# Three first additions of the closing stage move from VectorE to TensorE, and the last group's two loads signal apart

## What is computed

```python
x = x + xattn(ctx_1024, ctx_1024, layernorm(x), ...)      # softmax attention over 64 keys
def ffn(x, ...):                                          # E = 8 experts, K = 2, F = 512
    probs, idx = top_k(softmax(xt @ Wr + br), K)          # divided by their sum
    h = layernorm(relu(xt @ W1[e] + b1[e])) * g1 + be1
    y = layernorm(relu(h @ W2[e] + b2[e])) * g2 + be2
    out[t] = sum over k of gate[t, k] * y[idx[t, k], t]
x = x + ffn(layernorm(x), ...)
```

## Time and profile before

| what | us |
|---|---|
| median of 3 runs | 329.74 |
| lowest, highest run | 328.38, 334.85 |
| span of the profiled execution | 284.0 |
| TensorE, VectorE busy in the span | 240.0, 237.6 |
| ScalarE, POOL busy in the span | 215.7, 189.0 |

### The profile page before, as it was taken

How to read it: one execution, slowest core, us unless ns; L and a number is a source line. 1 busy time by engine, 2 the same in 40 slices (tenths; PEclk the granted TensorE clock), 3 DMA queues, 4 the chain that set the end, 5 groups by cost and what they waited for, 6 DMA issues and landing times.

```text
span 284.0 us, 10362 instructions
## 1 busy us (share of the span) xinstructions
PE 240.0 (84%) x2955; PEld 196.8 (69%) x2958; DVE 237.6 (84%) x1101; ACT 215.7 (76%) x799; POOL 189.0 (67%) x301
## 2 busy tenths in 40 slices
PE   1899779699798398769879999999999699889970
PEld 1474568567676244669768989999999599879520
DVE  0765986965997987778989899999999879889896
ACT  2544666779859867757799999999999789889820
POOL 8601277777667757827768777878887758677650
PEclk9977986999779759988999999999999999999997
DMA  6997398123424154351223333333235746452338
GB/s 162 336 265 256 77 270 261 48 86 102 124 77 158 49 85 104 80 133 48 60 51 67 78 69 69 58 80 77 61 78 152 142 132 141 125 141 58 106 117 289
DMA packets 48803, 34.59 MB, mean 122 GB/s; under 512 B 26934, under 2 KB 42870, under 8 KB 48747
## 3 DMA queue, kind: packets, MB, share of 16 engines
q1 hardware_dynamic: 39100, 22.83, 30.1%
q0 software_dynamic: 6592, 9.00, 11.9%
q10 hardware_dynamic: 3056, 2.11, 2.5%
HBM read 15.14 MB, written 12.02 MB: 96 GB/s over the span
## 4 chain that ended last, share of the span: by engine, by line
PE 22%; DVE 18%; issue 16%; POOL 14%; DMA 12%; ACT 8%; SPq 6%; POOLq 1%; DVEq 1%; ACTq 0%
PE bank L724 14%; POOL answers L682 9%; PE bank L728 7%; POOL words_of L708 5%; DMA w2f<-in_L_ffn_W 3%; DMA answers<-vo,words_of 3%; SPq L522 3%; DMA x_tok<-in_x 2%; DVE w2f L1668 2%; SPq L554 2%; DMA w_mean<-w_sums 1%; DMA kb_room<-slot_rows 1%; ACT ex L1175 1%; ACT xt L1198 1%; ACT rh L1347 1%
## 5 line engine op out<-in xcount | busy, mean ns | idle before, releaser
L682 POOL DMA_INDIRECT answers<-vo,words_of x71 | 70.1, 988 | 31.4 <-ACT vo L1389 18.5
L670 POOL DMA_INDIRECT slot_rows<-pay,pos x64 | 64.4, 1006 | 31.3 <-issue 18.1
L724 PE MATMUL bank<-kb_room,w1h 128*128 128x128 f16 x568 | 55.7, 220 | 8.9 <-DMA kb_room<-slot_rows 4.3
L728 PE MATMUL bank<-w2h,rh 128*128 x284 | 52.0, 221 | 2.1 <-DVE w2l L1675 1.6
L724 PEld LDWEIGHTS bank<-kb_room,w1h 128*128 x568 | 42.5, 98 | 15.7 <-issue 9.1
L728 PE MATMUL bank<-rh 128*128 128x129 f16 x284 | 52.1, 222 | 0.0
L728 PE MATMUL bank<-w2l,rh 128*128 x284 | 51.9, 221 | 0.0
L724 PE MATMUL bank<-kb_room,w1l 128*128 128x128 f16 x284 | 51.7, 221 | 0.0
L1347 ACT ACTIVATE rh<-bank 128x512 f16<-128x512 f32 x71 | 42.0, 591 | 12.3 <-PE bank L724 9.6
L1900 DVE SCALAR_TENSOR_TENSOR kq<-bank,rh 128x512 f16<-128x512 f32 x71 | 47.9, 674 | 0.1
L708 POOL DMA_DIRECT2D words_of<-slot_rows x71 | 40.5, 572 | 6.6 <-issue 4.5
(11 more groups left out here) (264 smaller groups left out, 608.3 us busy)
## 6 DMA issues: line engine op xcount, KB each, us to landing
x_tok<-in_x SPq DMA_DIRECT2D x8, 256.0 KB, 6.9
w1f<-in_L_ffn_W SPq DMA_DIRECT2D x2, 1024.0 KB, 9.2
pay<-pay SPq DMA_DIRECT2D x8, 256.0 KB, 2.9
w1f<-answers SPq DMA_DIRECT2D x8, 256.0 KB
w2f<-answers SPq DMA_DIRECT2D x8, 256.0 KB, 3.3
kb_room<-slot_rows SPq DMA_TRANSPOSE x71
words_of<-slot_rows POOLq DMA_DIRECT2D x71, 1.0 KB, 2.5
answers<-vo,words_of POOLq DMA_INDIRECT x71
```

Of the source, the lines that this page charges most:

```text
L670: eng.indirect_dma_start(slot_words, bass.IndirectOffsetOnAxis(ap=pos[:, g % 2, k, i:i + 1], axis=0), pay[g % 2][:, k, i, :].bitcast(U32), ...
L682: eng.indirect_dma_start(answers, bass.IndirectOffsetOnAxis(ap=words_of[:, j % NW, 0:1], axis=0), z[j % NZ], None).then_inc(s_ans[j % NZ], 16)
L724: return eng.matmul(dst, lhsT, rhs, start=start, stop=stop)
L728: return eng.matmul(dst, lhsT, rhs, start=start, stop=False, skip_group_check=True)
```

## The change

TensorE gets, for groups 2 to 4 (`FIRST_BY_PE`), a fourth product into their banks: identity by `ya[g][0]`, f32, 512 columns, behind a wait for the loads. VectorE's `with_first` isn't called for these groups; `with_second` adds the bank and the second answers. The first load of group 7 keeps its semaphore and the second gets one of its own, `s_back_last`: the first addition waits for the one, the halves for the other. The semaphore `s_digits`, its signal and TensorE's wait for it are removed.

```diff
-        s_place, p_place, s_tab, s_digits = (signal(n) for n in ("places", "pe_places", "tables", "digits_set"))
+        s_place, p_place, s_tab = (signal(n) for n in ("places", "pe_places", "tables"))
...
+        s_back_last = signal("back_last_second")
...
+        FIRST_BY_PE = (2, 3, 4)
...
             def answers_back(g):
                 for k in range(K):
-                    eng.dma_start(ya[g][k].rearrange("p (b q) d -> p b (q d)", q=2), ans_v[k, g]).then_inc(s_back[g], 16)
+                    eng.dma_start(ya[g][k].rearrange("p (b q) d -> p b (q d)", q=2), ans_v[k, g]).then_inc(
+                        s_back_last if g == GROUPS - 1 and k else s_back[g], 16)
...
                 if n == 0:
                     eng.wait_ge(s_xT, GROUPS)
-                    eng.wait_ge(s_digits, 1)
...
                 if g >= 2:
-                    t = mm(to, ident[:, :], group(x2, g)[:, :, 0:D], False, True)
+                    t = mm(to, ident[:, :], group(x2, g)[:, :, 0:D], False, g not in FIRST_BY_PE)
+                if g in FIRST_BY_PE:
+                    eng.wait_ge(s_back[g], 16 * K * (GROUPS - 2))
+                    t = mm(to, ident[:, :], ya[g][0], False, True)
                 t.then_inc(p_off, 1)
...
-                eng.tensor_reduce(digit_of[:, :], digits[:, :, :], AX.X, ALU.add).then_inc(s_digits, 1)
+                eng.tensor_reduce(digit_of[:, :], digits[:, :, :], AX.X, ALU.add)
...
+            def loaded(g, k):
+                eng.wait_ge(s_back[g], 16 * (K * (GROUPS - 2) if g < GROUPS - 2 else k + 1))
+
             def with_first(g):
                 eng.wait_ge(p_off, g + 1)
-                eng.wait_ge(s_back[g], 16 * K * (GROUPS - 2 if g < GROUPS - 2 else 1))
+                loaded(g, 0 if g == GROUPS - 1 else 1)
...
             def with_second(g, tiles):
-                eng.wait_ge(q_res, at[g])
-                eng.tensor_tensor(ya[g][1][:, tiles, :], ya[g][0][:, tiles, :], ya[g][1][:, tiles, :], ALU.add
+                if g in FIRST_BY_PE:
+                    eng.wait_ge(p_off, g + 1)
+                    loaded(g, 1)
+                    sums = offset_bank(g)[:, :].rearrange("p (i d) -> p i d", i=GT)
+                else:
+                    eng.wait_ge(q_res, at[g])
+                    if g == GROUPS - 1:
+                        eng.wait_ge(s_back_last, 16)
+                    sums = ya[g][0]
+                eng.tensor_tensor(ya[g][1][:, tiles, :], sums[:, tiles, :], ya[g][1][:, tiles, :], ALU.add
                                   ).then_inc(s_res, 1)
...
             for g in range(GROUPS - 2):
-                if g < GROUPS - 3:
+                if g < GROUPS - 3 and g + 1 not in FIRST_BY_PE:
                     with_first(g + 1)
                 with_second(g, slice(0, GT))
```

## The result

| kernel, runs of the first comparison | median us | lowest to highest |
|---|---|---|
| before, 4 runs | 331.6 | 328.38 to 334.85 |
| after, 4 runs | 333.54 | 333.25 to 334.09 |

The ratio after to before is 1.0108, with a 95% interval of 1.0062 to 1.0155. Forecast were 329.3 us and a range up to 331.7: the measured time lies above it, and the change is in the other direction. Ratios and their intervals leave out executions more than 1.5% above the fastest of their kernel, so a ratio need not be that of the medians (here 1.006).

A forecast was written before the change was run, and what follows sets the result against it. In the tail, VectorE's chain and the line of DMA transfers end together. VectorE loses 1.80 us, but the loads leave 0.4 off the span: 284.0 to 283.6, so 329.74 to 329.3 us; range 327.6 to 331.7.

The forecast's parts named there:

- 45.7 us: Distance of the 329.74 us median above the profiled span of 284.0, carried over unchanged in the sum.
- VectorE's order: Tail: three first additions leave VectorE, 1.80 us; group 6's second addition starts at 277.62, free for group 7 about 278.22.
- The products: Three f32 products join TensorE's tail at 0.96 us each; banks ready 0.10 to 0.37 us early for groups 5 to 7.
- Rivals A and D: A: loads not the limit, all 1.80 us off, 328.4, chance 0.12; D: TensorE half clock in tail, about 340, 0.01.
- The stores: Tail stores issued right behind second additions, from 273.42 to 278.34; groups 1 to 3 come 0.60 us apart.
- lands at the later of issue + 2.2 and the landing before + 0.68: Rule for the first four stores' landings in the tail: 275.6, 276.3, about 277.15 and 277.9.
- The loads: Group 7's loads, issued at 276.5 and 276.9, land by 279.3 to 279.6 and 280.0 to 280.5; halves about 280.5.
- the sign of being wrong: Halves starting later than 280.9, measured from the same point of the tile loop, would make the forecast wrong.
- The last scatter: POOL's last answer scatter stands behind the second store, releasing SyncE at about 276.5 instead of 276.04.
- rival C: Stores starve the last scatter; SyncE released about 277.8, halves 0.6 us later, 330.3 us; chance 0.17.
- The split signal: Separate semaphores for the last two loads: at most 0.14 us by itself before, mattering more after the change.
- Rival B: Queues take turns, stores share the loads' rate; second load at 280.7, 0.1 us won, 329.6; chance 0.12 including nothing won.

The follow-up runs named there:

- e8: Changed kernel with TensorE's three products left out, so first answers of groups 2 to 4 are missing from the output; tail 14.85 us.
- e13: Changed kernel repeated without edits, beside the unchanged one in the same job; ratio 0.9897 (0.9814 to 0.998), tail 15.02 us.
- e4: Kernel before with only the three products added, old semaphores kept; ratio 1.0214 (1.005 to 1.0377), tail 15.48 us.
- e6: Changed kernel with the stores of groups 2 to 6 held until the last load has landed; tail 15.66 us.
- e7: Changed kernel with group 7's second load issued from ScalarE's queue, behind the stores of groups 0 to 2; ratio 1.0171, tail 14.25 us.
- e12: Changed kernel with group 3's store and all later ones held until group 5's second addition is done; ratio 1.0015, tail 13.41 us.
- e2: Kernel before with only the digits' semaphore removed; ratio 1.0048 (0.999 to 1.0106), tail 13.74 us.
- e3: Changed kernel with no first addition on TensorE, keeping the last loads' two semaphores and the removed digits wait; ratio 1.0038, tail 13.52 us.
- e10: Changed kernel with only group 4's product on TensorE; tail 13.44 us.
- e11: Changed kernel with only the products of groups 3 and 4 on TensorE; tail 13.42 us.

## Why the prediction was wrong

**The total.** Four comparisons of the changed kernel gave 1.0108, 0.9986, 0.9984 and 0.9897. The first isn't repeated on either level, and the last, at the same level, goes the other way. The unchanged kernel against itself gave 1.0053 and 0.9937, the second with an interval that excludes 1. Over all executions the medians of the four comparisons stand at 1.006, 1.000, 1.000 and 0.999, and those of the unchanged kernel at 0.995 and 0.996. So the 3.6 us of the first comparison are for the most part scatter between executions: its four runs of before reached over 6.5 us. What the change does is in the tail, +0.8 us (median of four executions 14.39, of three unchanged 13.62), a quarter of a percent, not to be seen in a total. The forecast of no measurable change holds over all comparisons; its sign was wrong, and its range of 327.6 to 331.7 was too narrow for the scatter, of which three runs were known. Of the 4.2 us between 329.3 and 333.54, 1.9 lie in the base alone: with its fourth run the median of before was 331.6, not 329.74. That 45.7 us lie outside the span was wrong too, without effect on the sum.

**VectorE's order.** Right to 0.1 us: group 6's second addition at +7.35, forecast 277.62, which is +7.31.

**The products.** Too dear by 0.1 each: 0.86 instead of 0.96, bank 7 at +7.51 instead of +7.81. Their cover held, TensorE's wait for the loads cost nothing, and e8 shows that they are not on the path. Rivals A and D are out: VectorE idled 2.5 us for the loads, and the clock stayed at 1.00 until 328.

**The stores.** Issued when forecast. The step of the sum that failed is the rule "lands at the later of issue + 2.2 and the landing before + 0.68". It gave 5.3, 6.0, 6.8 and 7.6 for groups 0 to 3; the trace has 5.3, 6.4, 7.3 and 8.5. The 0.68 came from the full stretch at the end of before, where stores alone are served, at 384 GB/s. Around the last scatter it was 1.1 to 1.2 us: between the first two stores where the scatter's issue took 0.96, between the second and the third where it took 1.50 (e13: 5.3, 6.1, 7.3, 8.1). And where the line turns from stores to loads, the full engines move 250 GB/s, not 384. Before has such a stretch as well (277 to 278, share 0.94):

```profile
277.00:278.00 1.00, 0.00 (x0) 0.00 (x0) 1.00 (x2) 0.00 (x0) 0.00 (x0) 1.00 0.94 196
```

I took the rate of another stretch. Together the two make group 3's store 0.9 us late. What makes the rate low there wasn't tested.

**The loads.** Forecast at +9.0 to 9.3 and +9.7 to 10.2 (279.3 to 279.6, 280.0 to 280.5), landed at +9.8 to 10.2 and +11.1 to 11.3 in the executions without the long scatter. Most of this is the 0.9 us of group 3's store. From its landing to that of the second load the forecast had 2.1 to 2.6 us, for group 4's store and both loads, and it took 2.6. That group 4's store came between the loads, and not ahead of both as I had it, adds nothing to the second load; the forecast had counted it in front. The halves wait for the second load and start at +11.22 instead of +10.2, which is what turned 0.4 us won into 0.6 lost. It is also past the +10.6 (280.9) that the prediction named as the sign of being wrong.

**The last scatter.** I had SyncE released 0.5 us late every time. It was released 0.1 us late in three executions of after and 0.9 us late in one; counting e4 and e8, late in three of six with this order of stores, and in none of the seven with the second store at +4.3. That is rival C's late release in three of the six, with 0.5 to 0.7 us on the tail where it occurs, but not its mechanism: 0.5 of the 0.9 us is POOL's own issue of the scatter (1.50 us), and only 0.3 comes behind it. In e6, e7 and e12 the second store was as early and the issue took 0.96.

VectorE's rows narrow it down. The issue starts at +3.00, right behind an addition that starts at +2.99. Before, and in e2, e3, e10 and e11, that addition reads a bank. After the change it is the second addition of group 1, which reads two SBUF tiles, in all nine executions with the early second store. Either that addition takes 0.73 us instead of 0.69 and the issue 0.96 (six executions), or the addition takes 0.69 and the issue 1.50 (three). The rows of e13, against 319.60 and 1.34 for the pair in after:

```profile
313.67 1.29 DVE L2021 TENSOR_TENSOR w1f<-w1f 128x512 f32<-128x512 f32 x2
```

The scatter before the last is issued beside three such additions, and takes 1.44 or 1.45 us in all sixteen traces; no other scatter's issue takes more than 1.08. So the new order of the additions, and not only the earlier store, stands beside the long issue. No run separates the two, and why it falls the one way or the other stayed open.

**The split signal.** Right: after the change it is worth 0.7 us (e4), without the products nothing (e3).

**Rival C's outcome** (slower by 0.6, halves late, the end with them) is what the trace of after shows, by a different mechanism: not SyncE late, but the transfers slow. Rival B, by the rule of the Trainium skill ("DMA: Bandwidth & Descriptors", section "Queues, rings and completion order") that the queue rows are served in turn, also had the loads slowed by stores beside them. It gave +10.4 for the second load's landing, nearer to the +11.1 than my own. The landings of after (group 4's store, second load, group 5's store, 0.5 to 0.8 us apart) are in the order of issue, so they don't show it; e7's two loads, issued together on two queues and landing 0.5 apart after 4.1 and 4.6, would fit it.

## What to carry to other kernels

An engine that is made faster issues its stores earlier, and if a later load from the same DMA engines ends the program, they stand in its way: look at which transfers will be in front of the last load, and keep stores that nobody waits for behind it. When the engine's chain and the line of transfers end together, shortening the chain wins nothing even with the transfers in the best order (e12: halves 1.0 us earlier, end 0.1 to 0.3). And take a transfer's rate from the stretch in which it will run, not from the fullest one.

## What was not expected of the hardware

- One program has two levels, by the chip or by the job, medians of 281.5 to 282.3 and 328.9 to 333 us, with busy times within about 1 us on every engine but TensorE (591 ns for the activation in both) and a tail of 13.5 to 13.7 us at both.
- Full DMA engines moved 378 to 385 GB/s in stores, but 196 and 250 for a microsecond where stores gave way to loads from DRAM, and 157 for two where two loads were issued on two queues at once (e7, one execution).
- The same indirect scatter of 65 KB took POOL 0.96 or 1.50 us to issue, and the wait behind it ended 0.8 us later with the second. The long issue was seen only beside additions of two SBUF tiles.
